# An expert and attention kernel whose second-group sorts keep one row scatter under way at a time

## Chip, core and metric

The kernel runs on one core of a Trainium2 chip. The metric is the device time of one execution, in microseconds. A core has five engines that run their own instruction queues and meet only at semaphores: TensorE (PE in the profile, its weight loads PEld), VectorE (DVE), ScalarE (ACT), GpSimd (POOL) and SyncE (SP), which here only issues DMAs. DMAs are carried out by 16 DMA engines that all queues share.

## What is computed

A "macaron" block on x of shape 4 x 1024 x 128: a routed feed-forward layer at half weight, a linear attention with decay, and the same feed-forward layer again. The reference, cut:

```
def ffn(x):                       # 4096 tokens of 128, 8 experts, 512 hidden
    logits = xf @ Wr.T + br
    expert_idx = argmax(logits)
    h = relu(einsum('td,efd->etf', xf, W1) + b1)
    y = einsum('etf,edf->etd', h, W2) + b2
    return y[expert_idx, arange(tokens)]
x = x + 0.5 * ffn(layernorm(x))
x = x + attn(layernorm(x))        # q,k,v = silu(x W); 16 heads of 8, decay per head; norm, gate, Wo
x = x + 0.5 * ffn(layernorm(x))
```

The reference computes all experts for all tokens and picks one. The kernel computes only the picked one: each token's row goes to the tiles of its expert.

## The kernel before

There are two expert layers with the attention between them. The 4096 tokens are 32 tiles of 128; each layer treats them in two groups of 16 tiles, so there are four units u = 0 to 3, and u = 1 and 3 are each layer's second group.

*Sorting.* Once a unit's router has chosen, VectorE writes for each token the slot it goes to (`slot_of`). `sort_rows(u)` on GpSimd then issues 16 indirect DMAs, one for each tile of tokens (line 336). Each takes 128 rows of 272 floats from SBUF (the token's x, its normalised row and its number) and scatters them to their slots in `slots_in[u]`, in HBM. A unit has 23 tiles of slots (16 and room for every expert's last tile to be part full), filled beforehand with rows that name no token. Each DMA adds 16 to the semaphore `rows_sorted[u]` when it has landed.

*The expert pass.* Each layer handles 46 slot tiles G, 0 to 45 in layer 0 and 46 to 91 in layer 1. TensorE, in turn G, transposes tile G + 1 (line 945), multiplies tile G with the expert's first weights (953), and tile G - 1 with the second (963). ScalarE copies the transposed tile to SBUF (433) and does half of the hidden layer's bias and relu (448), VectorE the other half (730); VectorE adds the result to the row (737). GpSimd's `scatter` sends each finished tile's rows to their tokens with an indirect DMA (line 346). All waits between these engines are semaphores; each TensorE step is told by the last matmul of the step.

*Loads.* SyncE's queue is in the order of the tiles. In turn G it loads slot tile G + 6 into a ring of 24 (line 279, for tiles from 24 on after the scatter of the tile 24 before it), then the first weights of tile G + 3 into a ring of 4 (line 287, after product G - 1). The first slot tile of a unit waits for the unit's whole sort:

```
if first_of_unit(G):
    sp.wait_ge(rows_sorted[u], 16 * GROUP_TILES)
```

So slot tile 23 (loaded in turn 17) waits for sort 1, with the weights of tile 20 behind it, and slot tile 69 (turn 63) for sort 3, with the weights of tile 66 behind it.

*GpSimd's queue*, in the order of its program:

```
sort_rows(0)
sort_rows(1)
scatter(0, LAYER_TILES)
(the attention's outer products and state updates)
sort_rows(2)
scatter(LAYER_TILES, LAYER_TILES + EARLY_SCATTERS)
sort_rows(3)
scatter(LAYER_TILES + EARLY_SCATTERS, LAYERS * LAYER_TILES)
```

`LAYER_TILES` is 46 and `EARLY_SCATTERS` 6: sort 3 stands between the scatters of tiles 51 and 52, and is issued as soon as its routing, done inside the expert pass, is known.

Of the kernel before, what the change touches and what calls it, by code (L numbers as in the profile page):

```python
# [21 lines left out]
GROUPS = 2  # L22
# [44 lines left out]
def wait(eng, sem, value):  # L67
    if value > 0:
        eng.wait_ge(sem, value)
# [15 lines left out]
def build(nc, x, w1t, bias, w2t, wrt, br, wqkv, wg1t, wg2, wo, gamma, beta, decay, const, out):  # L85
    with ExitStack() as ctx:
# [85 lines left out]
        def cst(name, rows_=P):  # L172
            a, w = CONST[name]
            return const_sb[0:rows_, a:a + w]
# [28 lines left out]
        rows_sorted = by_unit("rows_sorted")  # L203
# [39 lines left out]
        def outer_product(eng, n, half, b):  # L243

            w = HEADS // 2
            at = b * 3 * D + half * w * HD
            k_ = qkv[n % 2][:, at + D:at + D + w * HD].unsqueeze(2).to_broadcast([P, w * HD, HD])
            v_ = (qkv[n % 2][:, at + 2 * D:at + 2 * D + w * HD].rearrange("p (h e) -> p h e", e=HD)
                  .unsqueeze(2).to_broadcast([P, w, HD, HD]))
            u_ = outer[n % 2][:, b * UW + half * w * UH:b * UW + (half + 1) * w * UH]  # L250
            return eng.tensor_tensor(u_.rearrange("p (h d e) -> p h d e", d=HD, e=HD),  # L251
                                     k_.rearrange("p (h d) e -> p h d e", d=HD), v_, ALU.mult)
# [68 lines left out]
        @block.gpsimd  # L321
        def _(pool):
            pool.memset(fill[:, 0:ID_AT], 0.0).then_inc(fill_ready, 1)
            pool.memset(fill[:, ID_AT + 1:ROW], 0.0).then_inc(fill_ready, 1)
            pool.memset(fill[:, ID_AT:ID_AT + 1].bitcast(I32), NO_TOKEN).then_inc(fill_ready, 1)
            pool.memset(rows_v[:, :, ID_AT + 1:ROW], 0.0).then_inc(ids_ready, 1)
            pool.memset(carry[:, :], 0.0).then_inc(carry_done, 1)

            def sort_rows(u):

                pool.wait_ge(rows_kept, (u + 1) * GROUP_STEPS)
                pool.wait_ge(ids_ready, 2)
                pool.wait_ge(slots_known[u], 1)
                pool.wait_ge(slots_filled[u], 16)
                for t in range(GROUP_TILES):
                    pool.indirect_dma_start(  # L336
                        slots_in[u], bass.IndirectOffsetOnAxis(ap=slot_of[u][:, t:t + 1], axis=0),
                        row_of(u % GROUPS * GROUP_TILES + t), None).then_inc(rows_sorted[u], 16)

            def scatter(first, end):  # L340

                for G in range(first, end):
                    pool.wait_ge(y_done, G + 1)
                    if G >= SCATTER_SEMS:
                        wait_scattered(pool, G - SCATTER_SEMS)
                    pool.indirect_dma_start(  # L346
                        x1 if layer_of(G) == 0 else out, bass.IndirectOffsetOnAxis(ap=ids_in_ring(G), axis=0),
                        in_ring(G, 0, D), None, bounds_check=NO_TOKEN - 1,
                        oob_is_err=False).then_inc(scattered[G % SCATTER_SEMS], 16)

            def decay_keys(n):

                pool.wait_ge(qkv_done, BATCH * (n + 1))
                wait(pool, delta_ready, n - 1)
                pool.tensor_tensor(per_batch(kd[n % 2][:, :]),
                                   qkv[n % 2][:, :].rearrange("p (b w) -> p b w", b=BATCH)[:, :, D:2 * D],
                                   cst("decay_k").unsqueeze(1).to_broadcast([P, BATCH, D]), ALU.mult).then_inc(kd_done, 1)

            def update_carry(n):

                pool.wait_ge(delta_copied, n + 1)
                pool.tensor_tensor(per_batch(carry_new[:, :]), per_batch(carry_new[:, :]),
                                   cst("carry_mask").unsqueeze(1).to_broadcast([P, BATCH, D]),
                                   ALU.mult).then_inc(delta_masked, 1)
                pool.wait_ge(delta_masked, n + 1)
                pool.wait_ge(carry_aged, n + 1)
                pool.tensor_tensor(carry[:, :], carry[:, :], carry_new[:, :], ALU.add).then_inc(carry_done, 1)

            def outer_products(n):

                pool.wait_ge(qkv_done, BATCH * (n + 1))
                wait(pool, state_ready, PAIRS * (n - 1))
                for h in range(2):
                    if n > 0 or h > 0:
                        for b in range(BATCH):
                            last = outer_product(pool, n, h, b)
                        last.then_inc(outer_done, 1)
# [4 lines that stand above are left out]
            for n in range(STEPS):  # L382
                outer_products(n)
                if n + 1 < STEPS:
                    decay_keys(n)
                if n > 0:
                    update_carry(n - 1)
# [4 lines that stand above are left out]
# [800 lines left out]
```

## Time and profile before

| what | value |
|---|---|
| median of 3 runs | 519.02 us (518.94 to 520.21) |
| the profiled execution | 516.73 us |
| its span, first to last instruction | 514.9 us |
| mean granted TensorE clock | 0.84 of full speed |
| TensorE busy | 369.8 us, 72% |
| VectorE busy | 326.6 us, 63% |
| GpSimd busy | 243.6 us, 47% |
| ScalarE busy | 190.3 us, 37% |
| layer 0's expert pass | about 60 to 180 us |
| attention | about 180 to 367 us |
| layer 1's expert pass | about 367 us to the end |

How to read it: a timeline row gives the start and the busy time of an instruction (or of several alike), and in brackets how long its engine sat idle before it and what ended that. "issue" is no wait that the profile shows, "remote" one whose end it can't name. A DMA instruction's busy time is that of its issue; the data lands later. SyncE's rows are marked SPq. The granted clock is a share of TensorE's full speed, 1.00 (2.4 GHz) or 0.50 (1.2 GHz).

### The profile page before, as it was taken

The numbers are of one execution on the slowest core, as the hardware profiler recorded it, in microseconds if no ns is written. First come the engines' busy times: TensorE is split into PE (matmuls) and PEld (weight loads), VectorE is DVE, ScalarE is ACT, GpSimd is POOL, SyncE is SP. The second block draws the span as 40 slices with busy tenths as digits, with TensorE's granted clock in tenths as the row PEclk, the third lists the DMA queues.
The fourth block names the chain that finished last, engine by engine and source line by source line (L and its number), as shares of the span: only waits on it lengthen the run. The fifth ranks groups of instructions, "written<-read, shape, count | busy, mean of one in ns | idle before, by whom it ended". The sixth has DMA issues, their size and how long they took to land. (4 is left out here: it accounts for less than half of the span.)

```text
span 514.9 us, 10079 instructions
## 1 busy us (share of the span) xinstructions
PE 369.8 (72%) x2474; PEld 326.2 (63%) x2474; DVE 326.6 (63%) x972; ACT 190.3 (37%) x570; POOL 243.6 (47%) x246
## 2 busy tenths in 40 slices
PE   4484105999999967967969779666499720699983
PEld 2474105999998745646658667555399620599983
DVE  4745002566657389999999998996666700256641
ACT  1160002555555512343544635402365200255540
POOL 1007771455544457637364582657131277245443
PEclk9655556999999979979899897868699975599998
DMA  8993454788886199000000000003566442277840
GB/s 252 364 390 111 147 175 144 225 246 238 231 279 210 42 296 284 1 1 0 1 1 0 1 1 2 0 32 113 182 194 182 139 150 83 79 206 228 243 127 6
DMA packets 55238, 72.17 MB, mean 140 GB/s; under 512 B 6831, under 2 KB 39884, under 8 KB 54928
## 3 DMA queue, kind: packets, MB, share of 16 engines
q1 hardware_dynamic: 46784, 53.95, 35.2%
q0 software_dynamic: 6016, 13.13, 6.9%
q10 hardware_dynamic: 2384, 4.46, 2.3%
q8 instruction: 23, 0.38, 0.3%
q14 instruction: 31, 0.25, 0.2%
HBM read 45.58 MB, written 27.75 MB: 142 GB/s over the span
## 5 line engine op out<-in xcount | busy, mean ns | idle before, releaser
L953 PE MATMUL bank<-slot_xT,w_ring 128*128 128x128 f32 x736 | 103.4, 283 | 14.2 <-issue 8.2
L953 PEld LDWEIGHTS bank<-slot_xT,w_ring 128*128 128x128 f32 x736 | 93.4, 198 | 16.7 <-issue 12.0
L336 POOL DMA_INDIRECT slots_in<-rows,slot_of x64 | 62.4, 975 | 76.8 <-DVE slot_of L695 58.2
L730 DVE TENSOR_SCALAR hT_b<-bank,b_cur 128x128 f32<-128x128 f32 x184 | 56.0, 347 | 45.2 <-PE bank L953 26.7
L1011 PE MATMUL bank<-outer_all,decay_sb 128*128 128x256 f32 x256 | 75.3, 423 | 8.8 <-DVE outer_all L251 4.5
L251 POOL TENSOR_TENSOR outer_all<-qkv 128x512 f32<-128x512 f32 x60 | 63.9, 1100 | 24.6 <-ACT qkv L476 24.6
L346 POOL DMA_INDIRECT out_x<-ring x46 | 44.7, 972 | 64.6 <-DVE ring L737 42.9
L963 PE MATMUL bank<-w_sb,hT_a 128*128 x368 | 59.5, 285 | 18.7 <-DVE ring L737 17.1
L346 POOL DMA_INDIRECT x<-ring x46 | 44.6, 971 | 55.9 <-issue 31.7
L1011 PEld LDWEIGHTS bank<-outer_all,decay_sb 128*128 128x128 f32 x256 | 51.2, 211 | 28.1 <-issue 10.8
L771 DVE TENSOR_REDUCE o_in<-qS 128x64 f32<-128x512 f32 x64 | 68.0, 1073 | 0.0
L448 ACT ACTIVATE hT_a<-bank,b_cur 128x128 f32<-128x128 f32 x184 | 57.4, 363 | 23.8 <-PE bank L953 16.0
L963 PEld LDWEIGHTS bank<-w_sb,hT_a 128*128 128x128 f32 x368 | 49.3, 195 | 22.0 <-issue 21.6
L723 DVE TENSOR_TENSOR ring<-ring,b_sb 128x128 f32<-128x128 f32 x92 | 26.9, 293 | 50.4 <-issue 38.4
L963 PE MATMUL bank<-w_sb,hT_b 128*128 x368 | 57.0, 278 | 0.0
L737 DVE SCALAR_TENSOR_TENSOR ring<-bank,ring 128x128 f32<-128x128 f32 x92 | 26.7, 290 | 43.7 <-remote 16.3
L433 ACT ACTIVATE slot_xT<-bank 128x128 f32<-128x128 f32 x92 | 25.1, 273 | 69.4 <-remote 55.7
L963 PEld LDWEIGHTS bank<-w_sb,hT_b 128*128 128x128 f32 x368 | 49.4, 195 | 0.0
L764 DVE TENSOR_TENSOR qS<-bank,qkv 128x512 f32<-128x512 f32 x64 | 43.5, 680 | 7.3 <-remote 3.9
L945 PE MATMUL bank<-const_sb,ring 128*128 128x128 f32 x92 | 26.4, 287 | 22.9 <-ACT slot_xT L433 22.6
L441 ACT ACTIVATE b_cur<-b_t 128x4 f32 x92 | 18.9, 205 | 62.9 <-DVE hT_b L730 47.0
L425 ACT ACTIVATE rnT<-bank 128x512 f32<-128x512 f32 x16 | 9.4, 595 | 56.6 <-PE bank L917 40.1
(110 smaller groups left out, 491.8 us busy)
## 6 DMA issues: line engine op xcount, KB each, us to landing
w_ring<-in_w1t SPq DMA_DIRECT2D x92, 256.0 KB
slots_in<-fill SPq DMA_DIRECT2D x4, 3128.0 KB, 18.3
ring<-slots_in SPq DMA_DIRECT2D x92, 136.0 KB
rows<-in_x SPq DMA_DIRECT2D x8, 256.0 KB, 6.6
w_sb<-in_w2t ACTq DMA_DIRECT2D x1, 2048.0 KB, 15.3
rows<-x SPq DMA_DIRECT2D x8, 256.0 KB, 4.3
decay_sb<-in_decay ACTq DMA_DIRECT2D x1, 1024.0 KB, 16.6
slots_in<-rows,slot_of POOLq DMA_INDIRECT x64
```

The source lines that it names most:

```text
L251: return eng.tensor_tensor(u_.rearrange("p (h d e) -> p h d e", d=HD, e=HD), k_.rearrange("p (h d) e -> p h d e", d=HD), v_, ALU.mult)
L336: pool.indirect_dma_start(slots_in[u], bass.IndirectOffsetOnAxis(ap=slot_of[u][:, t:t + 1], axis=0), row_of(u % GROUPS * GROUP_TILES + t), ...
L346: pool.indirect_dma_start(x1 if layer_of(G) == 0 else out, bass.IndirectOffsetOnAxis(ap=ids_in_ring(G), axis=0), in_ring(G, 0, D), None, b ...
L448: last = nc.scalar.activation(hT_a[G % 2][:, f * P:(f + 1) * P], bank_a[:, f * P:(f + 1) * P], ACT.Relu, bias=b1_cur[G % 2][:, f:f + 1])
L723: nc.vector.tensor_tensor(in_ring(G, 0, D), in_ring(G, 0, D), b2_sb[:, bass.ds(e, D)], ALU.add).then_inc(biased, 1)
L730: last = nc.vector.tensor_scalar(hT_b[G % 2][:, f * P:(f + 1) * P], bank_b[:, f * P:(f + 1) * P], b1_cur[G % 2][:, 2 + f:3 + f], 0.0, ALU. ...
L737: nc.vector.scalar_tensor_tensor(out=in_ring(G, 0, D), in0=y_bank[:, 0:D], scalar=0.5, in1=in_ring(G, 0, D), op0=ALU.mult, op1=ALU.add).th ...
L764: nc.vector.tensor_tensor(qS[h % 3][:, :].rearrange("p (b a e) -> p b a e", b=BATCH, e=HD), bank[h % 3][:, :].rearrange("p (b a e) -> p b ...
L771: nc.vector.tensor_reduce(o_in[:, h * w:(h + 1) * w].rearrange("p (a e) -> p a e", e=HD), qS[h % 3][:, :].rearrange("p (a d e) -> p a e d" ...
L953: last = mm(to[:, f * P:(f + 1) * P], w1_ring[G % W1_BUFS][:, (2 * half + f) * P:(2 * half + f + 1) * P], slot_xT[G % 2][:, :], start=True ...
L963: last = mm(y_bank[:, 0:D], h[:, f % 2 * P:(f % 2 + 1) * P], w2_sb[:, bass.ds(expert[G] + f * D, D)], start=(f == 0), stop=(f == FB - 1))
L1011: last = mm(to, decay_sb[:, (2 * h + a) * P:(2 * h + a + 1) * P], u, start=True, stop=True)
```

## The change

In `sort_rows`, for the second group of a layer (u = 1 and u = 3), each indirect DMA but the first waits until those before it have landed: `rows_sorted[u]` counts 16 for each. So in these two sorts one scatter is under way at a time. Sorts 0 and 2 and all else stay. The lines behind it move down by 3: the scatter of line 336 is line 339 after the change, that of line 346 is 349.

```
                 for t in range(GROUP_TILES):
+
+                    if u % GROUPS == 1 and t > 0:
+                        pool.wait_ge(rows_sorted[u], 16 * t)
                     pool.indirect_dma_start(
                         slots_in[u], bass.IndirectOffsetOnAxis(ap=slot_of[u][:, t:t + 1], axis=0),
                         row_of(u % GROUPS * GROUP_TILES + t), None).then_inc(rows_sorted[u], 16)
```

## Rows read from the trace of the kernel before

**Rows 1.** Page, group: busy us, mean ns, idle before, releaser.
```profile
L336 POOL DMA_INDIRECT slots_in<-rows,slot_of x64 | 62.4, 975 | 76.8 <-DVE slot_of L695 58.2
```

**Rows 2.** Windows: stretch, length, busy and count by engine, clock, DMA share, GB/s.
```profile
96.00:122.00 26.00, 26.00 (x233) 25.85 (x232) 15.79 (x56) 15.29 (x56) 12.81 (x15) 1.00 0.81 241
408.50:412.50 4.00, 3.13 (x21) 2.57 (x21) 2.86 (x13) 1.09 (x5) 3.09 (x4) 1.00 0.62 189
412.50:428.40 15.90, 3.17 (x17) 2.48 (x17) 0.90 (x3) 1.11 (x4) 12.21 (x13) 0.69 0.39 138
428.40:438.60 10.20, 0.00 (x0) 0.00 (x0) 0.00 (x0) 0.00 (x0) 7.79 (x8) 0.50 0.20 66
```

**Rows 3.** Timeline of GpSimd, layer 0: start, busy, instruction, idle before.
```profile
57.41 0.96 POOL L336 DMA_INDIRECT slots_in<-rows,slot_of  x1 [0.30 <-issue]
58.67 0.96 POOL L336 DMA_INDIRECT slots_in<-rows,slot_of  x1 [0.30 <-issue]
...
77.64 0.96 POOL L336 DMA_INDIRECT slots_in<-rows,slot_of  x1 [0.30 <-issue]
...
91.38 0.98 POOL L346 DMA_INDIRECT x<-ring  x1 [0.90 <-issue]
```

**Rows 4.** Timeline of SyncE, layer 0.
```profile
59.85 1.79 SPq L279 DMA_DIRECT2D ring<-slots_in  x4
65.89 0.72 SPq L287 DMA_DIRECT2D w_ring<-in_w1t  x1
```

**Rows 5.** Timelines of TensorE and ScalarE, layer 0's first tile.
```profile
62.03 0.48 PE L945 MATMUL bank<-const_sb,ring 128*128 128x128 f32 x1
...
83.56 1.93 PE L953 MATMUL bank<-slot_xT,w_ring 128*128 128x128 f32 x8
...
82.90 0.28 ACT L433 ACTIVATE slot_xT<-bank 128x128 f32<-128x128 f32 x1 [34.52 <-remote]
```

**Rows 6.** Timelines of GpSimd, SyncE, TensorE, VectorE around sort 3.
```profile
408.48 0.96 POOL L336 DMA_INDIRECT slots_in<-rows,slot_of  x1 [17.71 <-DVE slot_of L695]
...
427.40 0.96 POOL L336 DMA_INDIRECT slots_in<-rows,slot_of  x1 [0.30 <-issue]
...
437.62 0.97 POOL L346 DMA_INDIRECT out_x<-ring  x1 [0.30 <-issue]
...
429.85 0.32 SPq L279 DMA_DIRECT2D ring<-slots_in  x1
...
413.14 0.61 PE L963 MATMUL bank<-w_sb,hT_b 128*128 x4
413.59 0.27 PE L945 MATMUL bank<-const_sb,ring 128*128 128x128 f32 x1
...
442.95 0.44 PE L945 MATMUL bank<-const_sb,ring 128*128 128x128 f32 x1 [1.28 <-ACT slot_xT L433]
...
439.02 0.29 DVE L737 SCALAR_TENSOR_TENSOR ring<-bank,ring 128x128 f32<-128x128 f32 x1 [16.35 <-remote]
```

**Rows 7.** Timelines of GpSimd and TensorE near 490 us.
```profile
489.77 0.97 POOL L346 DMA_INDIRECT out_x<-ring  x1 [0.30 <-issue]
491.04 0.97 POOL L346 DMA_INDIRECT out_x<-ring  x1 [0.30 <-issue]
...
493.60 1.13 PE L953 MATMUL bank<-slot_xT,w_ring 128*128 128x128 f32 x8 [1.57 <-ACT hT_a L448]
```

**Rows 8.** Timeline of TensorE: first products of tile 20, of tile 66.
```profile
122.67 1.06 PE L953 MATMUL bank<-slot_xT,w_ring 128*128 128x128 f32 x8
...
452.70 1.06 PE L953 MATMUL bank<-slot_xT,w_ring 128*128 128x128 f32 x8
```

**Rows 9.** Chain that ended last, around 407 us: start, length, what.
```profile
407.44 0.17 DVE slot_of L695
```

**Rows 10.** Page, DMA issues: KB each, median us to landing.
```profile
rows<-in_x SPq DMA_DIRECT2D x8, 256.0 KB, 6.6
...
rows<-x SPq DMA_DIRECT2D x8, 256.0 KB, 4.3
```

More of the change, by code:

```diff
@@ L335, in sort_rows @@
                 for t in range(GROUP_TILES):
+                    if u % GROUPS == 1 and t > 0:
+                        pool.wait_ge(rows_sorted[u], 16 * t)
                     pool.indirect_dma_start(
```

## The prediction, made before the changed kernel had run

> **What bounds the kernel now.** I read the page first, then TensorE's, GpSimd's and the other engines' timelines side by side around the four sorts, then the table of windows.
>
> The page's group for the changed line has 64 row scatters (four sorts of 16) of 975 ns each, 62.4 us busy [rows 1]. In each sort they stand 0.30 us apart, so one starts every 0.96 + 0.30 = 1.26 us; the last of sort 0 starts at 57.41, the first of sort 1 at 58.67, its last at 77.64 [rows 3]. Sorts 1 and 3 overlap the expert pass, and that is where the trace is odd.
>
> Layer 0: sort 0 has landed by 59.85 (SyncE issues the first slot loads, which wait for it), 1.48 us after its last scatter's end at 58.37 [rows 3, 4]. TensorE transposes the first slot at 62.03, done at 62.51. ScalarE's copy of that result waits for nothing else, and starts at 82.90; the first product at line 953 starts at 83.56 [rows 5]. SyncE's one DMA instruction, 0.45 us at 59.85, takes 0.72 us at 65.89 [rows 4]. The stall ends 4.3 us after sort 1's last scatter (77.64 + 0.96 = 78.60).
>
> Layer 1: sort 3 starts at 408.48. In the first 4 us TensorE does 21 matmuls, in the next 15.9 us only 17, and in 428.4 to 438.6, while GpSimd sends backlogged output scatters just as close, none [rows 2]. VectorE's add at line 737 waits for products that ended at 413.14 + 0.61 = 413.75, and runs at 439.02; TensorE's transposes are at 413.59 and then 442.95 [rows 6], 4.4 us after the last close scatter (438.59). So, as a reading of these rows: **while GpSimd sends indirect DMAs 0.30 us apart, TensorE's semaphore signals arrive late and the expert pass stands**, after some microseconds in which it still runs. It is the closeness, not the kind: output scatters do it too, three of them in a row, the last two at 489.77 and 491.04, put the next product off to 493.60 [rows 7]. At the steady pace of one per 0.98 + 0.90 = 1.9 us [rows 3] TensorE is busy 26.00 of 26.00 us [rows 2].
>
> **The change.** It adds 15 waits to sort 1 and 15 to sort 3. Nothing else moves. Queued behind them: the rest of the sort and all row scatters of finished tiles (line 346). Waiting for the sort's last landing: SyncE at the first slot load of the second group, and behind it on SyncE's queue the weight loads.
>
> *Period of one waited scatter.* 0.96 us on GpSimd, then the landing, then GpSimd's start. Landing: 1.48 us after the end in [rows 3, 4], and 427.40 + 0.96 = 428.36 to 429.85, 1.49, in [rows 6]. Start after a wait: the slots are known at 407.44 + 0.17 = 407.61, the scatter starts at 408.48, 0.87 [rows 6, 9]; SyncE's 1.48 has some of this in it, so I take 3.2 for the sum of 3.3. That is quiet. Beside tile traffic (DMA share 0.81 [rows 2]) the landing has no row; its bounds are 1.5 (no effect) and 1.5 + 2.3 = 3.8, since a 256 KB load of the rows takes 6.6 us while the start's loads crowd the engines and 4.3 later [rows 10]. I take the middle, 2.9, so a period of 4.6 (3.2 to 5.6).
>
> A page of the Trainium skill would put the traffic's part at nothing: "DMA: Bandwidth & Descriptors", in the section on the anatomy of one DMA on the SWDGE path, fits 2.0 us plus bytes over 436 GB/s for one DMA, whatever runs beside it. With its 2.3 us and the 0.87 above, sort 1 would be some 11 us shorter, and the whole change about 10 us cheaper. The quiet rows agree with it (2.4 us from start to landing); no row tells the loaded case.
>
> *Layer 0.* Sort 1 starts at 58.67 as before. With GpSimd now idle most of the time, the close stretch ends at 58.4, and the pass should start when the weights are there: about 64.5 instead of 83.56, a gain of 19. It runs at 1.9 us a tile. But SyncE stops: in its turn 17 it wants slot 23, the second group's first, and stands until sort 1 has landed, with the weights of tile 20 behind it. Turn 16 comes at about 64.5 + 16 x 1.9 = 95; until then there is traffic. Scatter 1 starts at about 62.5, scatter 8 at 62.5 + 7 x 4.6 = 94.7, scatter 9 at 98.5, scatter 15 at 98.5 + 6 x 3.2 = 117.7; landed 120.2. Weights of tile 20 are issued some 1.3 us later and take about 2.5 (the smaller slot load of 59.85 is used at 62.03, 2.2 us [rows 4, 5]): product 20 at 124, where it is now at 122.67 [rows 8]. The 19 us are gone: **the wait for the sort takes their place**.
>
> Then comes the second bill. GpSimd has sent none of the scatters of tiles 0 to 18. From 118.9 it sends them 0.30 us apart (0.98 + 0.30 = 1.28 each), which is the pattern that stops the engines. I allow three more tiles before they stand, as the 4 us in [rows 2] do: 22 x 1.28 = 28, to 147, plus 4 to recover (4.3 and 4.4 above): 151. Tile 22's second products (line 963) would run then; now they are at 122.67 + 2.8 + 2 x 1.9 = 129.3. **+22** with the clock's restart (the first tiles run at the lower of two levels, as now after 83.56).
>
> *Layer 1.* Sort 3 starts at 408.48, beside traffic for its first two periods (4.0 taken, tiles are slower here), quiet for 13: last start 408.48 + 8 + 13 x 3.2 = 458.1, landed 460.5. The pass goes on instead of standing at 413.75, but only to tile 65: the weights of tile 66 stand behind the load of slot 69. Product 66 comes at about 464; now 452.70 [rows 8]. Backlog: tiles 52 to 64, 13, plus three: 16 x 1.28 = 20.5 from 459.4, to 480, plus 4: 484, for a tile (68) whose second products now are at 452.70 + 2 x 1.9 + 2.8 = 459.3, and the backlog's start is uncertain by a tile or two. **+23**.
>
> Sum: +45 us. On the profiled execution 516.73 + 45 = 562; the runs' median is 2.3 above it, so 519.0 + 45 = **564 us**.
>
> **Rivals.**
> *A, the catch-up does not stop the engines.* For it: the close stretch of sort 3 began with 4 us of normal work, and sort 0 runs beside the routing. Against: the stretch 428.4 to 438.6 is made of such scatters. Then layer 0 costs 124 - 122.67 + 1.5 for the restart = +3, layer 1 464 - 452.7 + 1.5 = +13: 519 + 16 = 535. In between lie partial stops, 535 to 550.
> *B, faster.* As A, and the landing is quick beside traffic too. With period p layer 0 changes by 58.67 + 15p + 2.4 + 3.8 + 1.5 - 122.7 = 15p - 56, layer 1 by 408.48 + 15p + 2.4 + 3.8 + 1.5 - 452.7 = 15p - 37. The sum is nil at p = 3.1, so below that the earlier start wins: at p = 2.7 it is -12, 507 us. The quiet rows already give 3.2.
> *C, the waits don't free the engines.* If indirect DMAs harm by being there and not by closeness, the pass stands until the sorts end: layer 0 58.67 + 15 x 3.2 + 1 + 4.3 = 112 instead of 83, +29; layer 1 408.48 + 49 + 4.4 = 462 instead of 443, +19: 519 + 48 = 567. The steady pace of 1.9 us speaks against it.
>
> **How the numbers follow.** Forecast 0.63 (548 to 582); A with partial stops 0.22; C 0.08; B and its neighbourhood around nil 0.07. The range of 8 in 10 leaves out B, the better part of A's low end and the longest periods: 530 to 584. Each microsecond of period is worth about 7 to 8 us in layer 0 beside traffic. A measurement of this kernel can tell about 0.3% (1.6 us) from no change. Slower by over 0.3%: 0.93; within: 0.02; faster: 0.05.
>
> **What would show it.** GpSimd's rows of sorts 1 and 3 start 3.2 us apart when quiet and 4 to 5 beside tiles; ScalarE's first copy at line 433 comes at about 63 instead of 82.90; TensorE stands before product 20 and product 66, waiting for weights whose issue follows the sort's landing; then GpSimd's scatters of line 346 come 0.30 us apart for some 20 us, and TensorE has an idle stretch under them in each layer. If TensorE keeps 1.9 us a tile under them, A holds. If ScalarE's first copy still comes after the sort, C holds. A sort 1 shorter than 45 us would bring B near.

## The result, and the profile after

| what | before | after |
|---|---|---|
| median | 518.98 us (516.84 to 520.21) | 556.3 us (552.55 to 560.59) |
| ratio of the times | | 1.0733, 95% interval 1.0676 to 1.0789 |
| the profiled execution | 516.73 us | 558.69 us |
| its span | 514.9 us | 556.8 us |

The change costs 37.3 us by the medians and 558.69 - 516.73 = 42.0 us between the profiled executions, on which the rows below rest. Slower, as forecast; 564 was predicted.

The page of after, the group of the row scatter (busy, mean ns, idle before) and its line of the DMA issues:

```profile
L339 POOL DMA_INDIRECT slots_in<-rows,slot_of x64 | 62.7, 979 | 137.7 <-DMA slots_in<-rows,slot_of 70.0
...
slots_in<-rows,slot_of POOLq DMA_INDIRECT x64, 2.4
```

The scatters cost GpSimd what they did in [rows 1]. Its idle time before them rose from 76.8 to 137.7 us, by 60.9: the 30 gaps that are now waits sum to 70.0 us, where they were 0.30 us each. That is GpSimd's own loss. What the kernel lost has to be read on TensorE.

**The sort of layer 0.** Timeline of GpSimd in after (start, busy, instruction, idle before and its releaser), from the first scatter of sort 1 to its last, and the output scatters behind it:

```profile
58.72 0.96 POOL L339 DMA_INDIRECT slots_in<-rows,slot_of  x1 [0.30 <-issue]
61.40 0.96 POOL L339 DMA_INDIRECT slots_in<-rows,slot_of  x1 [1.73 <-DMA slots_in<-rows,slot_of]
64.39 0.96 POOL L339 DMA_INDIRECT slots_in<-rows,slot_of  x1 [2.03 <-DMA slots_in<-rows,slot_of]
...
75.28 0.96 POOL L339 DMA_INDIRECT slots_in<-rows,slot_of  x1 [5.36 <-DMA slots_in<-rows,slot_of]
...
97.79 0.96 POOL L339 DMA_INDIRECT slots_in<-rows,slot_of  x1 [4.51 <-DMA slots_in<-rows,slot_of]
...
108.55 0.96 POOL L339 DMA_INDIRECT slots_in<-rows,slot_of  x1 [3.62 <-DMA slots_in<-rows,slot_of]
...
116.64 0.96 POOL L339 DMA_INDIRECT slots_in<-rows,slot_of  x1 [1.74 <-DMA slots_in<-rows,slot_of]
117.90 0.99 POOL L349 DMA_INDIRECT x<-ring  x1 [0.30 <-issue]
...
142.18 0.97 POOL L349 DMA_INDIRECT x<-ring  x1 [0.30 <-issue]
```

Quiet, a scatter and its wait take 0.96 + 1.73 = 2.69 us. Beside tiles the idle part is 2.0 to 5.4 us; the seven periods from 64.39 to 97.79 have a mean of 33.40 / 7 = 4.77. The sort that ended at 78.60 [rows 3] now ends at 117.60. Then 20 output scatters leave 1.28 us apart, 117.90 to 142.18.

ScalarE's first copy (against 82.90 in [rows 5]), SyncE around its wait for the sort, and TensorE's transposes (line 948) and first products (956):

```profile
63.37 0.28 ACT L436 ACTIVATE slot_xT<-bank 128x128 f32<-128x128 f32 x1 [14.95 <-PE bank L948]
...
97.59 0.34 SPq L287 DMA_DIRECT2D w_ring<-in_w1t  x1
119.07 0.32 SPq L279 DMA_DIRECT2D ring<-slots_in  x1
120.13 0.34 SPq L287 DMA_DIRECT2D w_ring<-in_w1t  x1
...
123.13 2.05 PE L956 MATMUL bank<-slot_xT,w_ring 128*128 128x128 f32 x8 [17.37 <-issue]
126.67 0.42 PE L948 MATMUL bank<-const_sb,ring 128*128 128x128 f32 x1
...
138.93 0.45 PE L948 MATMUL bank<-const_sb,ring 128*128 128x128 f32 x1 [1.30 <-issue]
...
146.30 2.05 PE L956 MATMUL bank<-slot_xT,w_ring 128*128 128x128 f32 x8 [6.93 <-ACT hT_a L451]
```

The pass starts 19.5 us earlier, runs to tile 19, and stands 17.4 us for weights that lie on SyncE's queue behind a slot load, which waits for the sort: product 20 runs at 123.13, against 122.67 in [rows 8]. Up to here the change costs half a microsecond. Then come the 20 close scatters, and TensorE passes two transposes (126.67, 138.93) in the time of twelve.

**The sort of layer 1**, GpSimd, SyncE and TensorE:

```profile
432.29 0.96 POOL L339 DMA_INDIRECT slots_in<-rows,slot_of  x1 [17.66 <-DVE slot_of L698]
434.98 0.96 POOL L339 DMA_INDIRECT slots_in<-rows,slot_of  x1 [1.73 <-DMA slots_in<-rows,slot_of]
...
473.42 0.96 POOL L339 DMA_INDIRECT slots_in<-rows,slot_of  x1 [1.73 <-DMA slots_in<-rows,slot_of]
474.68 0.99 POOL L349 DMA_INDIRECT out_x<-ring  x1 [0.30 <-issue]
...
490.02 0.97 POOL L349 DMA_INDIRECT out_x<-ring  x1 [0.30 <-issue]
...
475.87 0.32 SPq L279 DMA_DIRECT2D ring<-slots_in  x1
...
480.07 2.04 PE L956 MATMUL bank<-slot_xT,w_ring 128*128 128x128 f32 x8 [34.82 <-issue]
...
493.70 0.45 PE L948 MATMUL bank<-const_sb,ring 128*128 128x128 f32 x1
```

The same in the same order: TensorE works up to tile 65, stands 34.8 us for the sort, and then creeps under 13 close scatters. Three windows of after (stretch, length, busy and count of PE, weight loads, DVE, ACT, POOL, granted clock, DMA share, GB/s) put the three parts side by side; [rows 2] has before's:

```profile
66.00:96.00 30.00, 29.94 (x246) 29.31 (x247) 16.43 (x57) 15.87 (x58) 5.93 (x6) 0.93 0.81 254
124.00:148.00 24.00, 8.67 (x40) 7.96 (x40) 2.36 (x8) 2.57 (x10) 14.72 (x17) 0.57 0.33 105
474.00:492.00 18.00, 4.70 (x26) 4.55 (x27) 1.00 (x4) 0.83 (x3) 13.03 (x14) 0.69 0.48 144
```

Beside waited scatters TensorE is busy 29.94 of 30 us; under close output scatters 8.67 of 24 and 4.70 of 18 (of the 12 us that are left, counted from product 66 at 480.07).

### The profile page after: what moved, and what is told of

Read it like the earlier page. It is cut to its first block and busy times, and to the rows that moved or that the text cites. A ratio compares the mean times of both kernels' runs of the same rounds, so it can differ in the third digit from the quotient of the medians.

```text
span 556.8 us, 10079 instructions
## 1 busy us (share of the span) xinstructions
PE 378.6 (68%) x2474; PEld 334.9 (60%) x2474; DVE 327.6 (59%) x972; ACT 190.0 (34%) x570; POOL 243.7 (44%) x246
## 5 line engine op out<-in xcount | busy, mean ns | idle before, releaser
L956 PE MATMUL bank<-slot_xT,w_ring 128*128 128x128 f32 x736 | 107.7, 291 | 67.6 <-issue 52.2
L956 PEld LDWEIGHTS bank<-slot_xT,w_ring 128*128 128x128 f32 x736 | 97.5, 205 | 70.9 <-issue 65.6
L339 POOL DMA_INDIRECT slots_in<-rows,slot_of x64 | 62.7, 979 | 137.7 <-DMA slots_in<-rows,slot_of 70.0
L966 PE MATMUL bank<-w_sb,hT_a 128*128 x368 | 61.5, 292 | 16.9 <-DVE ring L740 8.4
L966 PEld LDWEIGHTS bank<-w_sb,hT_a 128*128 128x128 f32 x368 | 51.5, 202 | 20.0 <-issue 19.8
L966 PE MATMUL bank<-w_sb,hT_b 128*128 x368 | 58.9, 285 | 0.0
L966 PEld LDWEIGHTS bank<-w_sb,hT_b 128*128 128x128 f32 x368 | 51.4, 202 | 0.0
L926 PEld LDWEIGHTS bank<-wr_sb,rnT 128*128 128x128 f32 x128 | 25.1, 293 | 6.6 <-ACT rnT L428 6.5
```

Of the source, the lines that this page charges most:

```text
L339: pool.indirect_dma_start(slots_in[u], bass.IndirectOffsetOnAxis(ap=slot_of[u][:, t:t + 1], axis=0), row_of(u % GROUPS * GROUP_TILES + t), ...
L956: last = mm(to[:, f * P:(f + 1) * P], w1_ring[G % W1_BUFS][:, (2 * half + f) * P:(2 * half + f + 1) * P], slot_xT[G % 2][:, :], start=True ...
L966: last = mm(y_bank[:, 0:D], h[:, f % 2 * P:(f % 2 + 1) * P], w2_sb[:, bass.ds(expert[G] + f * D, D)], start=(f == 0), stop=(f == FB - 1))
```

## Experiments

Times are medians, ratios are to the kernel before, run on the same chip beside them (517.2, 518.9 and 519.2 us in the three sets e1 to e4, e5 to e8, e9 to e12). "Paced" means that GpSimd clears a tile that nobody uses ahead of an indirect DMA, so that starts lie further apart with no wait:

```
def pace(width):
    wait(pool, gap_done, gapped[0])
    pool.memset(gap[:, 0:width], 0.0).then_inc(gap_done, 1)
    gapped[0] += 1
```

### One layer at a time

```
-                    if u % GROUPS == 1 and t > 0:
+                    if u == 1 and t > 0:      # e1; e2: u == 3
                         pool.wait_ge(rows_sorted[u], 16 * t)
```

> The wait only in sort 1 (layer 0); sort 3 as before. The two traces put layer 0's share at 366.1 - 342.3 = 24 us (start of sort 2) and layer 1's at the rest of 42. If the two layers' bills are separate: about 519 + 24 = 543 us. If layer 0's delay is partly given back in layer 1: under 535.

> The wait only in sort 3 (layer 1). Separate bills: about 519 + 18 = 537 us. GpSimd's scatters of line 336 in sort 3 stand 2.7 us apart, TensorE stands from about 414 to 458 and again under the scatters that follow 0.30 us apart.

Measured: e1 538.78 us, ratio 1.0424 (1.0376 to 1.0472); e2 536.43 us, 1.0379 (1.0333 to 1.0424). That is +21.6 and +19.2, together 41, against +37 for both (each with an interval of some 2.5 us either way). e1 lies 4 us below what was expected, e2 on it. There are two separate bills, one per layer, and within the intervals they add up.

### Is it the wait, or the catch-up behind it?

e4 is the changed kernel with the output scatters paced after each sort (1.65 us apart in place of 1.28); e3 is the kernel before with its sorts 1 and 3 paced, and no wait.

```
+                    if G < 30 or 52 <= G < 81:      # e4, ahead of each output scatter
+                        pace(480)
...
-                    if u % GROUPS == 1 and t > 0:   # e3, in sort_rows
-                        pool.wait_ge(rows_sorted[u], 16 * t)
+                    if u % GROUPS == 1 and t > 0:
+                        pace(480)
```

> The changed kernel, but with the same small clear before each output scatter of tiles 0 to 29 and 52 to 80, so that the catch-up too comes 1.9 us apart. Theory closeness: TensorE does not stand under the catch-up; from product 20 and product 66 it keeps 1.9 us a tile, and the layers end with GpSimd's backlog instead: 517 + 18 in layer 0 (last scatters 0.30 apart after TensorE is done) and + 10 in layer 1, near 547 us. If the idle stretch under the catch-up has another cause (the ring of slots, the landing order), it stays and the time rises above the changed kernel's 556.

> No wait for a landing: in sorts 1 and 3 GpSimd clears a small unused tile before each scatter, so that they start about 1.9 us apart instead of 1.26. Theory closeness: the expert pass runs beside the sorts (ScalarE's first copy at 63 instead of 83, TensorE keeps its 1.9 us a tile up to tile 20 and tile 65), and the bill is only the catch-up of some 14 scatters in each layer: layer 0 about -3, layer 1 about +5, near 521 us. Theory presence (row scatters harm by being there, whatever their spacing): the pass still stands until the sorts end, 10 us later in each layer, near 539 us.

e4: 544.04 us, 1.0536 (1.0470 to 1.0602), 12 us less than the changed kernel. The wait is all there, with product 20 at 120.41; what is gone is the creeping. The starts came 1.65 us apart, and not the 1.9 that was expected. GpSimd and TensorE in e4 just behind the wait:

```profile
120.58 0.97 POOL L359 DMA_INDIRECT x<-ring  x1 [0.17 <-POOL gap L335]
122.23 0.97 POOL L359 DMA_INDIRECT x<-ring  x1 [0.16 <-POOL gap L335]
...
128.16 0.27 PE L958 MATMUL bank<-const_sb,ring 128*128 128x128 f32 x1
...
130.06 0.27 PE L958 MATMUL bank<-const_sb,ring 128*128 128x128 f32 x1
...
162.51 2.05 PE L966 MATMUL bank<-slot_xT,w_ring 128*128 128x128 f32 x8 [9.83 <-issue]
```

A transpose every 1.9 us under scatters 1.65 us apart, where the changed kernel has one in twelve. The last row is a third bill, which the creeping had covered. SyncE in e4:

```profile
154.79 2.03 SPq L292 DMA_DIRECT2D rows<-x  x4
...
158.11 0.35 SPq L289 DMA_DIRECT2D w_ring<-in_w1t  x1
```

In turn 32 SyncE loads back the rows of the first group, for which all 23 of its output scatters must have landed. The late, paced catch-up sends the 23rd at 151.93, and the weights of tile 35 stand behind that load: TensorE waits 9.8 us for them. So the catch-up costs by its closeness or, without it, by its lateness. e4 isn't free of closeness either: its scatters from tile 30 on are unpaced, five of them leave close behind the last paced one (164.73 to 169.84), and TensorE runs no transpose between 167.82 and 175.42. By the start of sort 2, 359.30 against 342.31, layer 0 still costs 17.0 us in e4; 10.7 of the 27.7 us between the profiled executions are layer 1's.

e3: 513.46 us, 0.9923 (0.9888 to 0.9958), a little faster than before, and 8 us under the 521 that was expected. With sort 1 paced the first copy comes at 70.98 in place of 82.90, but five output scatters that have piled up then leave close (84.12 to 89.25), and no transpose runs between 86.11 and 93.89.

### Pacing everything, half as wide, and only the output scatters

e5 paces sorts 1 and 3 as e3, and every output scatter too; e6 is e5 with `pace(224)`; e7 paces the output scatters alone.

```
                 for G in range(first, end):
+                    pace(480)                 # e5, e7; e6: pace(224)
                     pool.wait_ge(y_done, G + 1)
```

> As e3 (a small clear before each scatter of sorts 1 and 3), and the same clear before every output scatter, so that no indirect DMA of GpSimd after sort 0 and 2 starts less than 1.65 us after the one before. Theory closeness: e3's two remaining idle stretches of TensorE (86 to 94 in layer 0, 442 to 452 in layer 1) go, and with them 6 to 8 us in layer 0 and about 10 in layer 1: about 513 - 16 = 497 us. If the expert pass is held by something else at those points (the landing of slots, the ring): within 3 us of e3's 513.

> e5 with a clear of half the width, about 1.43 us from start to start. If the limit lies below 1.43, TensorE still runs unhindered and the sorts end 3 us earlier each: 491 to 495 us. If it lies between 1.43 and 1.65, idle stretches come back beside the sorts: 500 us or more.

> The kernel before, with the clear before the output scatters alone; all sorts stay 1.26 us apart. Layer 0 as before (its first copy still after sort 1, about 83 us). Layer 1: the stretch 428 to 439, eight output scatters 0.30 apart, is paced, so the pass should resume about 4 us after sort 3's last scatter instead of after theirs: 433 instead of 443, and the short stall near 490 goes: 517 - 10 = 507 us. If the stall is the row scatters' own doing and outlasts them anyway: 515 or more.

e5: 500.53 us, 0.9654 (0.9604 to 0.9704), where 497 was expected. e6: 514.98 us, 0.9932 (0.9904 to 0.9961). e7: 513.35 us, 0.9907 (0.9870 to 0.9944), less of a gain than expected and between the two cases written down: sort 3 stays close, and the transposes at 416.68 and 437.32 have nothing between them. The first rows of the paced sort 1 in e6, ScalarE's first copy, and two of TensorE's transposes beside sort 3:

```profile
60.55 0.97 POOL L347 DMA_INDIRECT slots_in<-rows,slot_of  x1 [0.16 <-issue]
...
61.98 0.97 POOL L347 DMA_INDIRECT slots_in<-rows,slot_of  x1 [0.17 <-issue]
...
81.84 0.28 ACT L445 ACTIVATE slot_xT<-bank 128x128 f32<-128x128 f32 x1 [33.02 <-remote]
...
425.15 0.42 PE L957 MATMUL bank<-const_sb,ring 128*128 128x128 f32 x1
...
433.09 0.42 PE L957 MATMUL bank<-const_sb,ring 128*128 128x128 f32 x1
```

Starts 1.43 us apart leave the copy at 81.84, where it was before; starts 1.65 us apart (e3, e5) bring it to 71. In layer 1, beside sort 3 at the same 1.43 us (408.86 to 430.32) and the output scatters behind it, TensorE creeps: its transposes are at 414.08, 420.04, 425.15, 433.09 and 446.14. So the bound between harmless and harmful spacing lies between 1.43 and 1.65 us in this kernel.

### The bytes

The kernel before, with sort 3 sending 80 of each row's 272 floats to another tensor in HBM (the rows of layer 1's second group aren't delivered, that part of the output is left out).

```
-    slots_in[u], ..., row_of(...), None)
+    slots_in[u] if u < 3 else narrow, ..., row_of(...)[:, 0:ROW if u < 3 else 80], None)
```

> The kernel before, but sort 3 sends only the first 80 of each row's 272 floats, and to another place in HBM, so that the last unit's slots hold filler rows and name no token: this part of the output is left out. 16 DMAs 0.30 us apart as before, with under a third of the bytes. Theory closeness (the number of them counts): TensorE stands from about 413 as before, for as long, within 3 us of before (517). Rival, the bytes that they move: the stall shrinks by half or more, 507 or less.

517.52 us, 1.0023 (0.9979 to 1.0066). With 80/272 of the bytes and the same closeness, TensorE:

```profile
415.35 0.27 PE L947 MATMUL bank<-const_sb,ring 128*128 128x128 f32 x1
...
441.04 0.45 PE L947 MATMUL bank<-const_sb,ring 128*128 128x128 f32 x1 [1.28 <-issue]
```

No transpose between 415.35 and 441.04, as between 413.59 and 442.95 in [rows 6] (from 430.52 on under output scatters, whose bytes are as before). The DMA engines' share beside the sort fell from 0.39 (413.60 to 427.00, before) to 0.16 (415.40 to 428.00, e8), and the stall stayed: it isn't the bytes. Every scatter in these runs has 128 rows, so a price by the row isn't ruled out.

### How many under way, or how close

The kernel before, with sorts 1 and 3 waiting for the scatter two before (even and odd ones count on their own semaphores; SyncE waits for both).

```
+                    if u % GROUPS == 1 and t > 1:
+                        pool.wait_ge((rows_sorted, rows_odd)[t % 2][u], 16 * (t // 2))
```

> The kernel before with a wait in sorts 1 and 3 for the scatter two before (even and odd scatters count on their own semaphores), so that two are under way at a time. From the waited period of 2.7 us quiet the starts should lie 1.27 and 1.42 us apart in turn, mean 1.35. Theory A (what holds TensorE's signals is how close the scatters are issued, limit between 1.43 and 1.65 us): quiet it stays under the limit, the stall stays and the time is near the kernel before, 512 to 520. Theory B (what holds them is how many scatters are under way): with two at most the pass runs during the sorts at a period of about 2.1 us, sort 3 takes 34 us, and the time lies between the kernel before and the changed one, or below both: 505 to 530 with first copies near 63 us.

514.41 us, 0.9938 (0.9895 to 0.9980). GpSimd in sort 3, and TensorE's transposes beside it:

```profile
416.37 0.96 POOL L343 DMA_INDIRECT slots_in<-rows,slot_of  x1 [0.47 <-DMA slots_in<-rows,slot_of]
417.64 0.96 POOL L343 DMA_INDIRECT slots_in<-rows,slot_of  x1 [0.31 <-issue]
419.05 0.96 POOL L343 DMA_INDIRECT slots_in<-rows,slot_of  x1 [0.46 <-DMA slots_in<-rows,slot_of]
420.32 0.96 POOL L343 DMA_INDIRECT slots_in<-rows,slot_of  x1 [0.31 <-DMA slots_in<-rows,slot_of]
...
418.71 0.27 PE L953 MATMUL bank<-const_sb,ring 128*128 128x128 f32 x1
...
426.07 0.42 PE L953 MATMUL bank<-const_sb,ring 128*128 128x128 f32 x1
...
433.26 0.42 PE L953 MATMUL bank<-const_sb,ring 128*128 128x128 f32 x1
```

Two at most are under way, 1.32 us apart in these rows ((431.07 - 408.37) / 15 = 1.51 over the whole sort), and TensorE creeps at 7.3 us a tile, where in before it stood. e6 creeps in the same way, at 1.43 us and with no limit on how many are under way, so the spacing is enough to account for it. In layer 0, where traffic stretched the starts to 2.2 us apart on average, the first copy came at 67.32 and the pass ran.

This run doesn't part closeness from the number under way. A quiet scatter lands about 2.4 us after its start, so starts 1.26 us apart have two under way as well, and the limit of two hardly binds. The case for closeness comes from e9 below, by an estimate: beside layer 0's tiles a waited scatter took 3.9 to 6.4 us from start to start in after, so scatters 1.65 us apart there should be two to four under way, and TensorE is busy 30.00 of 30 us. No row shows the landings of the paced scatters, so this stays an estimate.

### What is left in the best version

e9 is e5 with six clears between sorts 0 and 1; e10 is e5 with slot tiles loaded 4 turns ahead in place of 6; e12 is e5 with sort 2 paced too.

```
+            for _ in range(6):
+                pace(480)
             sort_rows(1)
...
-            SLOTS_AHEAD, W1_AHEAD, X1_AT = 6, 3, 32
+            SLOTS_AHEAD, W1_AHEAD, X1_AT = 4, 3, 32
...
-                    if u % GROUPS == 1 and t > 0:
+                    if u > 0 and t > 0:
                         pace(480)
```

> The all-paced kernel with six more clears of 480 columns (0.4 us each with their gap) on GpSimd between sort 0 and sort 1, so that sort 1 begins some 2.5 us later. In the paced kernel ScalarE's first copy comes only near 71 us though sort 1 has been paced since 58; in the changed kernel it comes at 63.4. Theory A (a backlog left by sort 0's close scatters has to drain, and a pause drains it): the first copy comes at 62 to 65, the pass starts 6 us earlier, sort 1 lands 2.5 us later; since layer 0's tile 20 waits for that landing anyway only part is kept: 494 to 500. Theory B (the late first copy belongs to the spacing of 1.65 us itself): copy stays near 71, time 500 to 503.

> The all-paced kernel with slot tiles loaded 4 turns ahead in place of 6, so that SyncE's wait for sort 3 stands in turn 65 and the weights of tile 68 are behind it in place of those of tile 66 (in layer 0 of tile 22 in place of 20). In the paced kernel TensorE's transposes stand from 413.8 to 436.0 for the landing of sort 3. If that wait is what is left in layer 1, two more tiles of about 2 us each move ahead of it: 496 to 499. If slot loads 4 turns ahead come too late elsewhere, the time rises by what each is late: 501 to 510.

> The all-paced kernel with sort 2 paced too (start to start 1.65 us in place of 1.26). Sort 2 gets 15 x 0.39 = 6 us longer, and layer 1's pass can't start before its landing. If TensorE's attention work beside sort 2 is held by close scatters as the pass is, some of that comes back. Expected without that: +4 to +6 us on the all-paced kernel, 504 to 507; with it: 498 to 503.

**e9: 494.40 us, 0.9538 (0.9489 to 0.9588)**, the fastest version here: 25 us under the kernel before, 62 under the changed one. ScalarE's copy and GpSimd in e9:

```profile
54.55 0.96 POOL L347 DMA_INDIRECT slots_in<-rows,slot_of  x1 [0.30 <-issue]
55.51 3.29 POOL L335 MEMSET gap<- 128x480 f32 x6
59.10 0.96 POOL L347 DMA_INDIRECT slots_in<-rows,slot_of  x1 [0.30 <-issue]
...
59.71 0.28 ACT L447 ACTIVATE slot_xT<-bank 128x128 f32<-128x128 f32 x1 [14.20 <-PE bank L959]
```

A pause of 3.6 us behind sort 0's close scatters, and the first copy waits for nothing but its transpose (at 71.48 in e5, with the same spacing in sort 1). The first product runs at 63.25, when its weights have come. The rows read as if something piled up under close scatters and had to drain, in some 12 us at a spacing of 1.65 us and within a pause of 3.6 us; what that would be no run shows. The window of e9 beside its sort 1 and catch-up, with GpSimd nearly full and TensorE full:

```profile
66.00:96.00 30.00, 30.00 (x255) 29.60 (x254) 16.94 (x59) 16.13 (x60) 27.03 (x37) 0.96 0.90 287
```

e9's profiled sort 0 began 2.8 us earlier than e5's for reasons that the edit can't have, so its spans (490.9 against 498.9) flatter it; the medians give 6 us.

e10: 499.43 us, 0.9632 (0.9592 to 0.9671). That is 1 us under e5, which is no difference clear of the noise, though TensorE's last transpose comes 6 us sooner (476.04 against 481.77). The last output scatter starts at 491.06 in place of 492.54.

In the paced kernels GpSimd is the bound of layer 1: from the end of sort 3 (427.40 in e5) its 40 output scatters follow each other almost without a gap, (492.54 - 427.40) / 39 = 1.67 us each. A spacing between 1.43 and 1.65 us, or an earlier sort 3, should shorten that chain; neither was tried.

e12: 506.78 us, 0.9753 (0.9723 to 0.9783), +6.3 on e5, just what sort 2 is longer. The attention gets nothing back.

## Why the prediction was right, point by point

**The mechanism.** *Close indirect DMAs on GpSimd hold the expert pass, and the waits free it.* Right: the first copy came at 63.37, "about 63" was written. Rival C, that the pass stands until the waited sorts end, is out by the same row. e3, e5 and e9 show it without any wait, e6 shows that a little spacing isn't enough. The means that I named, semaphore signals that arrive late, is still only a reading of the rows: no run tells it from other causes.

**The wait takes the place of the stall.** Product 20 was put at 124, 1.3 us later than before; it ran at 123.13. The sort's last scatter was put at 117.7, and started at 116.64. Beside tiles 4.6 us a period was taken and 4.77 measured (the first two were 2.68 and 2.99). Quiet 3.2 was taken and 2.69 measured. That error didn't show here by luck: the six periods from 97.79 to 116.64, counted quiet, had one of 4.58 among them (103.97 to 108.55) and a first one of 3.50, mean 3.14.

**The period, quiet.** The mis-sized term. I added 0.87 us for GpSimd's start after a wait to the 1.48 of the landing. All of it together is 1.73 us in the rows above. The 1.48 was read at SyncE's own start, which holds one start already, and the 0.87 of [rows 9, 6] belongs to another releaser: VectorE's write of the slots, not a DMA. In layer 1 this made 13 x 0.5 = 6.5 us (6.1 in the rows, where two of the periods were longer).

**The period, beside traffic.** The middle between no effect and [rows 10] was close for layer 0 (4.6 against 4.77, with 3.9 to 6.4 for single ones). The Trainium skill, "DMA: Bandwidth & Descriptors", in the section on the anatomy of one DMA on the SWDGE path, fits 2.0 us plus bytes over 436 GB/s and has no term for what runs beside. Quiet, this trace agrees: the profile's page of after has 2.4 us as the median of the 64, against 2.3 by the fit. Beside layer 0's tiles it doesn't: the idle part alone reaches 5.36 us. In layer 1 the traffic's part was again small: sort 3's first periods are 2.69 and 2.95, where 4.0 was taken.

So the step from "beside tiles" to a longer period holds for seven periods of layer 0, but it isn't shown that the load on the DMA engines makes it. Single periods of after, as windows (DMA share second to last):

```profile
61.40:64.39 2.99, 1.46 (x14) 0.45 (x6) 0.59 (x2) 0.53 (x3) 0.96 (x1) 0.50 0.81 240
103.97:108.55 4.58, 1.79 (x17) 1.55 (x15) 1.56 (x6) 1.31 (x5) 0.96 (x2) 1.00 0.11 34
434.98:437.93 2.95, 2.73 (x23) 2.35 (x22) 1.88 (x7) 1.35 (x6) 0.96 (x2) 1.00 0.71 211
```

At shares of 0.81 and 0.71 a period was within 0.3 us of the quiet 2.69, and at 0.11 one took 4.58 us. That 4.6 came out as the mean in layer 0 is in part luck.

**Layer 0, the catch-up.** 22 close scatters and a recovery were put at 20.7 us beyond the wait; sort 2 started at 342.31 before and at 366.06 after, 23.8 later, so 23.3 came behind product 20:

```profile
366.06 1.02 POOL L339 DMA_INDIRECT slots_in<-rows,slot_of  x1 [5.07 <-DVE slot_of L698]
```

Not 22 but 20 scatters were close, as the rows above show; the creeping advanced two tiles and not three, and the first product behind it came 146.30 - 143.15 = 3.2 us after the last scatter's end.

**Layer 1.** +23 predicted, 42.0 - 23.8 = 18.2 measured. Product 66 was put 11.3 us later than before and ran at 480.07, which is 480.07 - 23.8 - 452.70 = 3.6 later: the sort took 473.42 - 432.29 = 41.1 us and not the 49.6 of the forecast, 6.1 of it by the quiet period and 2.4 by the first two. The catch-up then cost 18.2 - 3.6 = 14.6, against 11.7. So a wait that I had made too dear and a catch-up that I had made too cheap offset each other in part.

**The sum.** +45 was forecast, +42.0 measured in the profiled execution; the medians say +37.3, since the profiled execution of after lies 2.4 us above its median and that of before 2.3 below. The terms as written give a little more than the sum: 151 - 129.3 = 21.7 for layer 0, to which the clock's restart was to be added, and 484 - 459.3 = 24.7 for layer 1, put down as +23.

Rival A was out (TensorE does not keep its pace under the catch-up), but e4 prices most of it: with a paced catch-up the change costs +27, not the +16 worked out. By layer it is 17.0 against 3, and 10.7 against 13. In layer 0 product 20 even ran 2.3 us earlier than before, at 120.41; what A had left out is behind it, the 9.8 us that TensorE waits behind SyncE's turn 32, and the five close scatters that e4 leaves unpaced. Neither was in the forecast.

Rival B fails in layer 0 and in the sum. Its quiet period of 2.7 us did come true; the mistake to avoid would have been to use it beside layer 0's tiles.

## What to carry to other kernels

Waiting for each landing throttles a queue by the landing's latency, some 2.7 us quiet and 4.8 beside layer 0's tiles here, where spacing of 0.4 us was all that the other engines needed; and it piles up what stands behind it, which then leaves as close as it can. Before adding a wait to space an engine's work, try to space it with something of fixed length, and space the catch-up too. And read who waits for the *whole* of a slowed sequence: here a queue in order (SyncE's) turned the sort's last landing into a stop for weights that have nothing to do with it.

## What the runs showed of the hardware

- In this kernel 128-row indirect DMAs from GpSimd hold the other engines when they start 1.26 to 1.43 us apart, and don't at 1.65 us. Five in a row are enough (e3, 84.12 to 89.25: no transpose from 86.11 to 93.89), and 20 in a row held TensorE to two transposes in 24 us. A cut of the bytes to 80/272 changed nothing; fewer rows in a scatter weren't tried.
- The hold outlasts its cause: 12 us at a spacing of 1.65 us (first copy at 71 in e3 and e5), nothing to be seen after a pause of 3.6 us (59.71 in e9).
- What inside the chip is held stays open. The rows show instructions that run late with "issue" or "remote" before them, and none of the runs says more.
- A waited row scatter of 136 KB takes 2.69 us from start to start when nothing runs beside it (once 3.12, at 464.92), and 3.9 to 6.4 us in seven periods beside layer 0's tiles. What stretches it is open: the DMA engines' share doesn't tell the long periods from the short ones.
